# Attention's last body and the stretch behind it, with and without identity products

## The chip, the cores and the metric

The kernel runs on one core of a Trainium2 chip. The metric is device time in microseconds. Three runs of the kernel before took 544.23, 541.16 and 542.5 us, with a median of 542.5 us. The engines are PE (TensorE), DVE (VectorE), ACT (ScalarE), POOL (GpSimd) and SP, which issues most of the DMAs.

## The reference, cut to what matters

```python
def reference(x, ...):                                # x: [8, 256] token ids, width 192
    h = tok_ref(x)                                    # embedding, single-head mixer, MLP, two norms
    h = h + attn_ref(layernorm(h))                    # 12 heads of 16
    h = h + ffn_ref(layernorm(h))                     # two-level soft mixture of 8 x 4 experts

def attn_ref(x):
    qkv = (x @ qkv_w.T + qkv_b).reshape(B, N, 3, H, D).transpose(2, 0, 3, 1, 4)
    q, k, v = rms_norm(qkv[0], q_norm_w), rms_norm(qkv[1], k_norm_w), qkv[2]
    w = softmax(einsum('bhnd,bhmd->bhnm', q, k) / sqrt(D))
    out = einsum('bhnm,bhmd->bhnd', w, v).transpose(0, 2, 1, 3).reshape(B, N, C)
    return out @ proj_w.T + proj_b
```

## The kernel before, in words

Everything is in float32. The program is three blocks, one after the other: the token mixer with the attention (`mixer_and_attention`), the slots and the dispatch of the mixture (`slots_and_dispatch`), and the 32 experts (`experts`). Every engine has its own instruction list, written out by hand, and the engines meet at semaphores. Between two blocks all five engines wait for each other.

The attention works through the 8 sequences in 8 bodies (`body(n)`, n from 0 to 7). A sequence has 12 heads, in three quads of four. For each half quad PE makes a product of queries and keys for the row maxima (L615), DVE takes the maxima out of it (L1152), and PE makes the scores (L622), whose maximum is already taken off by a 17th row. PE turns the maxima (L637), ACT takes the exponentials (L927 for one half quad and L931 for the other), and PE mixes the values with them (L654). A product's banks are free again only when DVE or ACT has read them, so one group of products follows the next at the pace of DVE's maxima or ACT's exponentials. In bodies 0 to 6, PE fills that time with the front of a later sequence. In body 7 no later sequence is left.

Behind body 7 comes a tail for sequence 7 alone. It is one chain: scores, exponential, scores, exponential, mix (L654), copy on ACT (L936), six transposes (`turn_out`, L664), division on DVE (L1164 and L1168), four transposes (`turn_mixed`, L673), copy on ACT (L941), the output projection (`project`, L683), and the residual sum and its statistics on DVE and ACT (L1175 to L1186, L947 and L950).

SP's list has one duty at the end of the block. It waits for the last projection and for three other semaphores, and then clears 53 semaphores one by one (L100). After that it joins the other engines at the end of the block (L117).

`keep_busy` (L108 to L111) issues products of the identity matrix with itself, 128 by 128, into a bank that nobody reads. A float32 product is two instructions on PE. `warm(n, first, last)` issues `first` of them in body 0 and `last` of them in body 7. Other calls stand in the mixer (18), ahead of body 0 (11), between the steps of the tail (4, 4, 4, 4, 3 and 10) and in the next block (3, 16 and 4): 107 products in all.

The next block begins on PE with three transposes (`turn(0)`, L1448), three identity products, three transposes (`turn(1)`), and the logits of sequence 0 (L1466, 16 instructions).

Of the kernel before, what the change touches and what calls it, by code (L numbers as in the profile page):

```python
# [22 lines left out]
BATCH, SEQ, DIM = 8, 256, 192  # L23
# [84 lines left out]
def keep_busy(nc, g, bank, count):  # L108

    for _ in range(count):  # L110
        nc.tensor.matmul(g.ps[bank][:, 0:P], g.ident[:, :], g.ident[:, :], start=True, stop=True)  # L111


def mixer_and_attention(nc, g):

    g.next_stage()
    with ExitStack() as ctx:  # L117
# [60 lines left out]
        def norms(i, which):  # L178

            return 2 * i + which + 1  # L180
# [36 lines left out]
        MAXES, SCORES, OUT, FRONT = (0, 1), (2, 3), (4, 5), (6, 7)  # L217
# [151 lines left out]
        def _(pe):  # L369
# [271 lines left out]
            def mix(n, q):  # L641
                pe.wait_ge(S["exped"], 2 * (QUADS * n + q) + 2)
                if q == 0:
                    pe.wait_ge(S["v_kept"], n + 1)
                    if n:
                        pe.wait_ge(S["divided"], n)
                if q == 2 and n == 0:
                    pe.wait_ge(tok["stats_kept"], norms(LAST, 1))
                if q == 2 and n:
                    pe.wait_ge(S["added"], n)  # L650
                bank = g.ps[OUT[q // 2]]
                for m in range(TPS):
                    for j in range(QH):
                        last = nc.tensor.matmul(  # L654
                            bank[32 * j:32 * j + 32, (q % 2) * SEQ:(q % 2 + 1) * SEQ],
                            val[n % 2][:, m, QH * q + j, :], prob[j // 2][:, j % 2, m, :],
                            start=(m == 0), stop=(m == TPS - 1))
                last.then_inc(S["mixed"], 1)

            def turn_out(n):  # L660
                pe.wait_ge(S["out_kept"], n + 1)
                for t in range(TPS):
                    for q in range(QUADS):
                        last = nc.tensor.transpose(g.ps[OUT[t]][:, q * P:(q + 1) * P],  # L664
                                                   out_t[:, q, t * P:(t + 1) * P], g.ident[:, :])
                last.then_inc(S["out_turned"], 1)

            def turn_mixed(n):
                pe.wait_ge(S["divided"], n + 1)
                flat_mixed = mixed[:, :, :, :].rearrange("p t h d -> p t (h d)")  # L670
                for c in range(2):
                    for t in range(TPS):
                        last = nc.tensor.transpose(  # L673
                            g.ps[OUT[1]][0:HALF, c * SEQ + t * P:c * SEQ + (t + 1) * P],
                            flat_mixed[:, t, c * HALF:(c + 1) * HALF], g.ident[:, :])
                last.then_inc(S["mixed_turned"], 1)

            def project(n):
                pe.wait_ge(S["mixed_kept"], n + 1)
                for t in range(TPS):  # L680
                    for c in range(2):
                        k = HALF + c
                        last = nc.tensor.matmul(g.ps[OUT[1]][:, t * DIM:(t + 1) * DIM],  # L683
                                                mixed_t[0:k, c, t * P:(t + 1) * P],
                                                g.t["proj_t"][0:k, c, :], start=(c == 0), stop=(c == 1))
                last.then_inc(S["projected"], 1)

            def warm(n, first, last):

                if n == 0 and first:  # L690
                    pe.wait_ge(tok["stats_kept"], norms(LAST, 1))
                    keep_busy(nc, g, OUT[1], first)
                if n == BATCH - 1 and last:
                    keep_busy(nc, g, FRONT[0], last)

            def body(n):
                fill, stat, prev = n + 1 < BATCH, n + 2 < BATCH, n > 0
# [8 lines left out]
                else:  # L706
                    pe.wait_ge(S["fill_kept_s"], 2 * n + 2)
                warm(n, 0, 5)
                scores_and_maxima((n - 1, 2, 1) if prev else None, nxt(0))
                if fill:  # L710
                    make_qk_rest(n + 1)
                warm(n, 0, 3)
                turn_max(n, 0)
                warm(n, 2, 0)
                if prev:
                    mix(n - 1, 2)
# [50 lines left out]
            for n in range(BATCH):  # L767
                body(n)
            scores_and_maxima((BATCH - 1, 2, 0), None)
            keep_busy(nc, g, 0, 4)  # L770
            scores_and_maxima((BATCH - 1, 2, 1), None)
            keep_busy(nc, g, 0, 4)
            mix(BATCH - 1, 2)
            keep_busy(nc, g, 0, 4)
            turn_out(BATCH - 1)
            keep_busy(nc, g, 0, 4)
            turn_mixed(BATCH - 1)
            keep_busy(nc, g, 0, 3)
            project(BATCH - 1)
            keep_busy(nc, g, 0, 10)  # L780

        @block.scalar
        def _(act):
# [1578 lines left out]
```

## Time and profile before

| | |
|---|---|
| median of three runs | 542.5 us |
| the three runs | 544.23, 541.16, 542.5 us |
| profiled execution, its own time | 544.31 us |
| its span, first to last instruction | 542.5 us |
| mean granted TensorE clock | 0.994 |
| PE busy | 514.5 us (95%) |
| DVE busy | 315.8 us (58%) |
| ACT busy | 252.8 us (47%) |
| POOL busy | 103.1 us (19%) |

The attention's bodies run from about 117 us of the span to 257.9 us, the tail to 269.2 us. The next block's first instruction starts at 273.14 us, the experts' at 397.88 us. The profiled execution takes 1.8 us more than its span, which is the time ahead of the first instruction and behind the last. A busy PE in the profile includes the identity products.

### The profile page before, as it was taken

How to read it: one execution, taken by the hardware profiler on the slowest of the kernel's cores; microseconds unless marked ns; L12 is line 12 of the kernel's file. 1: busy time of each engine (PE TensorE's matmuls, PEld its weight loads, DVE VectorE, ACT ScalarE, POOL GpSimd, SP SyncE). 2: the span in 40 equal slices, each digit the busy share in tenths (PEclk: the TensorE clock that was granted, in tenths of full speed). 3: DMA queues.
4: the chain of work that ended last, by engine and by line, in shares of the span. 5: the costliest groups of instructions: out<-in, count | busy, mean ns of one | idle time of the engine just before them, and what ended most of it. 6: DMA issues, size and time to landing. Idle time of an engine off the chain costs nothing. (4 is left out here: it accounts for less than half of the span.)

```text
span 542.5 us, 13583 instructions
## 1 busy us (share of the span) xinstructions
PE 514.5 (95%) x5421; PEld 422.2 (78%) x5421; DVE 315.8 (58%) x743; ACT 252.8 (47%) x823; POOL 103.1 (19%) x189
## 2 busy tenths in 40 slices
PE   6999999999999999999978899899989999999996
PEld 5888888965565566666867664588889999999985
DVE  3348679677767767755227866577723444434443
ACT  1244343456566567644347658757732322323220
POOL 6380000021042144041223760000100000000000
PEclk9999999999999999999989999899999999999999
DMA  6190000000000000000074000600059999899733
GB/s 246 29 316 3 2 0 1 2 1 1 1 1 2 1 1 1 2 2 1 1 306 160 2 2 2 234 1 2 1 221 408 314 359 383 319 325 310 196 53 123
DMA packets 20722, 58.80 MB, mean 108 GB/s; under 512 B 3042, under 2 KB 9796, under 8 KB 20548
## 3 DMA queue, kind: packets, MB, share of 16 engines
q1 hardware_dynamic: 14756, 49.47, 24.7%
q0 software_dynamic: 1056, 4.33, 4.2%
q10 hardware_dynamic: 4848, 4.13, 2.6%
q8 instruction: 43, 0.70, 0.6%
q14 instruction: 19, 0.16, 0.1%
HBM read 53.21 MB, written 4.33 MB: 106 GB/s over the span
## 5 line engine op out<-in xcount | busy, mean ns | idle before, releaser
L1152 DVE TENSOR_REDUCE qk<-banks 128x4 f32<-128x1024 f32 x48 | 58.8, 1225 | 39.5 <-PE banks L615 39.5
L2092 PE MATMUL banks<-slots_t,w 64*128 64x128 f32 x1344 | 80.7, 272 | 1.1 <-PEq L1323 1.1
L2092 PEld LDWEIGHTS banks<-slots_t,w 64*128 64x128 f32 x1344 | 79.1, 188 | 1.5 <-issue 1.3
L615 PE MATMUL banks<-qk_t 16*128 16x256 f32 x384 | 54.4, 400 | 2.6 <-DVE qk L1152 2.4
L622 PE MATMUL banks<-qk_t 17*128 17x256 f32 x384 | 54.4, 400 | 0.0
L615 PEld LDWEIGHTS banks<-qk_t 16*128 16x128 f32 x384 | 33.2, 184 | 20.3 <-issue 13.7
L2195 DVE TENSOR_REDUCE tokens<-banks 128x192 f32<-128x384 f32 x32 | 17.8, 557 | 47.2 <-PE banks L2123 47.2
L931 ACT ACTIVATE wk_t<-banks 128x512 f32<-128x512 f32 x48 | 26.1, 595 | 32.8 <-PE banks L622 32.8
L355 POOL TENSOR_TENSOR qk<-qk,att_rms 128x384 f32<-128x384 f32 x14 | 11.4, 837 | 150.6 <-ACT att_rms L903 150.6
L2165 ACT ACTIVATE yn_t<-banks,b_sb 128x128 f32<-128x128 f32 x64 | 18.3, 368 | 45.3 <-PE banks L2092 45.3
L2165 ACT ACTIVATE tokens<-banks,b_sb 128x128 f32<-128x128 f32 x64 | 18.3, 369 | 44.7 <-PE banks L2092 44.7
L927 ACT ACTIVATE wq_t<-banks 128x1024 f32<-128x1024 f32 x24 | 24.6, 1025 | 26.0 <-PE banks L622 25.6
L2123 PE MATMUL banks<-w,yn_t 64*128 64x192 f32 x384 | 35.3, 323 | 1.0 <-DVE yn_t L2185 1.0
L622 PEld LDWEIGHTS banks<-qk_t 17*128 17x128 f32 x384 | 32.8, 184 | 1.0 <-DVE qk_t L1157 0.4
L2123 PEld LDWEIGHTS banks<-w,yn_t 64*128 64x128 f32 x384 | 30.8, 187 | 1.2 <-issue 1.2
L111 PE MATMUL banks<-ident 128*128 128x128 f32 x214 | 28.1, 279 | 0.0
L111 PEld LDWEIGHTS banks<-ident 128*128 128x128 f32 x214 | 25.5, 192 | 2.6 <-issue 2.6
L2185 DVE SCALAR_TENSOR_TENSOR yn_t<-banks,b_sb,tokens 128x128 f32<-128x128 f32 x64 | 18.0, 344 | 16.1 <-ACT tokens L2165 16.1
L2214 POOL DMA_DIRECT2D yn_all<-rows_scratch x7 | 3.5, 500 | 120.7 <-DMA rows_scratch<-tokens 120.7
L2185 DVE SCALAR_TENSOR_TENSOR yn_t<-banks,b_sb,yn_t 128x128 f32<-128x128 f32 x64 | 18.0, 344 | 13.0 <-ACT yn_t L2165 13.0
L654 PE MATMUL banks<-wq_t,val 128*32 128x256 f32 x192 | 25.4, 385 | 0.1
L654 PE MATMUL banks<-wk_t,val 128*32 128x256 f32 x192 | 25.4, 385 | 0.0
(251 smaller groups left out, 1128.6 us busy)
## 6 DMA issues: line engine op xcount, KB each, us to landing
w<-in_w SPq DMA_DIRECT2D x28, 768.0 KB, 10.6
w<-in_w2e SPq DMA_DIRECT2D x24, 384.0 KB, 11.9
yn_t<-in_w SPq DMA_DIRECT2D x4, 768.0 KB, 10.3
yn_t<-in_w2e SPq DMA_DIRECT2D x8, 384.0 KB, 12.5
rows_scratch<-tokens ACTq DMA_DIRECT2D x28, 96.0 KB, 7.5
yn_all<-rows_scratch POOLq DMA_DIRECT2D x7, 384.0 KB, 9.8
w<-in_w_slot SPq DMA_DIRECT2D x4, 576.0 KB, 8.9
w_slot<-in_w_slot SPq DMA_DIRECT2D x3, 576.0 KB, 5.7
```

Of the source, the lines that this page charges most:

```text
L111: nc.tensor.matmul(g.ps[bank][:, 0:P], g.ident[:, :], g.ident[:, :], start=True, stop=True)
L615: last_best = nc.tensor.matmul(g.ps[MAXES[hh]][:, half * SEQ:(half + 1) * SEQ], g.qk_t[bn_ % 2][row:row + HDIM, bq, 0, half * P:(half + 1) ...
L622: last_score = nc.tensor.matmul(g.ps[SCORES[hh]][:, half * SEQ:(half + 1) * SEQ], g.qk_t[n % 2][row:row + HDIM + 1, q, 1, half * P:(half + ...
L654: last = nc.tensor.matmul(bank[32 * j:32 * j + 32, (q % 2) * SEQ:(q % 2 + 1) * SEQ], val[n % 2][:, m, QH * q + j, :], prob[j // 2][:, j % ...
L927: nc.scalar.activation(prob[u][:, :, :, :].rearrange("p a b n -> p (a b n)"), flat(SCORES[0], SCORES[1] + 1), ACT.Exp).then_inc(S["exped"], 1)
L931: nc.scalar.activation(prob[u][:, hh, :, :].rearrange("p b n -> p (b n)"), g.ps[SCORES[hh]][:, :], ACT.Exp).then_inc(S[done], 1)
L1152: nc.vector.tensor_reduce(to, flat(MAXES[0], MAXES[1] + 1).rearrange("p (h t n) -> p h t n", h=2, n=SEQ), AX.X, ALU.max, negate=True).then ...
L2092: return nc.tensor.matmul(bank[:, j * P:(j + 1) * P], g.w1[n % BUFS][rows, first + j * P:first + (j + 1) * P], x, start=start, stop=stop, ...
L2123: last = nc.tensor.matmul(out_bank(n, half)[:, 0:DIM], act_t[n % 2][rows, j * P:(j + 1) * P], g.w2[e][rows, j, :], start=(j == 0), stop=(j ...
L2165: nc.scalar.activation(gelu[n % 2][:, j * P:(j + 1) * P], gate_bank(n)[:, j * P:(j + 1) * P], ACT.Gelu_apprx_tanh, bias=g.t["b1"][:, n, HB ...
L2185: nc.vector.scalar_tensor_tensor(out=act_t[n % 2][:, j * P:(j + 1) * P], in0=value_bank(n)[:, j * P:(j + 1) * P], scalar=g.t["b1"][:, n, j ...
L2195: nc.vector.tensor_reduce(rows[n % ROWS][:, :], g.psum[:, first:first + 2, 0:DIM].rearrange("p b d -> p d b"), AX.X, ALU.add).then_inc(S[" ...
```

## The change

`warm` no longer issues anything in body 7, and the six calls of `keep_busy` in the tail are gone. The products in body 7 were 5, 3, 2, 2 and 4 (16 products), those of the tail 29. So 45 of the 107 identity products are left out, 90 instructions on PE with their weight loads. The other 62 stay, the three in the next block among them. No other engine's list changes, and no wait is added or removed. What the kernel computes is unchanged.

```diff
                 if n == 0 and first:
                     pe.wait_ge(tok["stats_kept"], norms(LAST, 1))
                     keep_busy(nc, g, OUT[1], first)
-                if n == BATCH - 1 and last:
-                    keep_busy(nc, g, FRONT[0], last)
...
             for n in range(BATCH):
                 body(n)
             scores_and_maxima((BATCH - 1, 2, 0), None)
-            keep_busy(nc, g, 0, 4)
             scores_and_maxima((BATCH - 1, 2, 1), None)
-            keep_busy(nc, g, 0, 4)
             mix(BATCH - 1, 2)
-            keep_busy(nc, g, 0, 4)
             turn_out(BATCH - 1)
-            keep_busy(nc, g, 0, 4)
             turn_mixed(BATCH - 1)
-            keep_busy(nc, g, 0, 3)
             project(BATCH - 1)
-            keep_busy(nc, g, 0, 10)
```

PE's list at the start of body 7, before. L615 and L622 are the products for maxima and scores, L637 turns the maxima, and L111 is `keep_busy`:

```order
L622 MATMUL banks<-qk_t 128x256 x2
L111 MATMUL banks<-ident 128x128 x5
L615 MATMUL banks<-qk_t 128x256 x2
L622 MATMUL banks<-qk_t 128x256 x2
L615 MATMUL banks<-qk_t 128x256 x2
L622 MATMUL banks<-qk_t 128x256 x2
L111 MATMUL banks<-ident 128x128 x3
L637 MATMUL banks<-ident,qk 128x128 x2
```

The same place with the change:

```order
L622 MATMUL banks<-qk_t 128x256 x2
L615 MATMUL banks<-qk_t 128x256 x2
L622 MATMUL banks<-qk_t 128x256 x2
L615 MATMUL banks<-qk_t 128x256 x2
L622 MATMUL banks<-qk_t 128x256 x2
L637 MATMUL banks<-ident,qk 128x128 x2
```

Two rows of identity products are gone, and the groups on either side of them stand next to each other, in the old order.

PE's list from the end of the last mix over the end of the block (L117) into the next block, before:

```order
L654 MATMUL banks<-wk_t,val 32x256 x2
L111 MATMUL banks<-ident 128x128 x4
L664 MATMUL banks<-ident,wv_t 128x128 x6
L111 MATMUL banks<-ident 128x128 x4
L673 MATMUL banks<-ident,w 96x128 x4
L111 MATMUL banks<-ident 128x128 x3
L683 MATMUL banks<-proj_t_sb,xt 128x192 x4
L111 MATMUL banks<-ident 128x128 x10
L117 UNCONDITIONAL_BRANCH
L1438 UNCONDITIONAL_BRANCH
L1448 MATMUL banks<-ident,tokens 128x128 x3
L111 MATMUL banks<-ident 128x128 x3
```

The same place with the change, where the next block's lines have moved up by eight:

```order
L654 MATMUL banks<-wk_t,val 32x256 x2
L664 MATMUL banks<-ident,wv_t 128x128 x6
L673 MATMUL banks<-ident,w 96x128 x4
L683 MATMUL banks<-proj_t_sb,xt 128x192 x4
L117 UNCONDITIONAL_BRANCH
L1430 UNCONDITIONAL_BRANCH
L1440 MATMUL banks<-ident,tokens 128x128 x3
L111 MATMUL banks<-ident 128x128 x3
```

Between the projection and the next block's first transposes PE now has nothing to do.

## Rows read from the trace of the kernel before

**Rows 1.** The page: TensorE's granted clock in 40 slices, in tenths.
```profile
PEclk9999999999999999999989999899999999999999
```

**Rows 2.** The identity products' line: duration in ns as min/median/max.
```profile
L111 PE MATMUL banks<-ident x214: 272/275/377, 90.4 to 393.3; 128*128 128x128 f32 x107
```

**Rows 3.** Timeline, start of body 7: start, duration, engine, instructions, [idle before <-releaser].
```profile
241.15 1.38 PE L111 MATMUL banks<-ident 128*128 128x128 f32 x10
241.25 1.23 DVE L1152 TENSOR_REDUCE qk<-banks 128x4 f32<-128x1024 f32 x1 [0.31 <-PE banks L615]
...
242.62 0.48 PE L615 MATMUL banks<-qk_t 16*128 16x256 f32 x2
```

**Rows 4.** Timeline of the tail and the border to the next block.
```profile
259.04 1.02 ACT L927 ACTIVATE wq_t<-banks 128x1024 f32<-128x1024 f32 x1 [2.28 <-PE banks L622]
...
260.12 1.13 PE L622 MATMUL banks<-qk_t 17*128 17x256 f32 x8
...
264.43 0.87 PE L664 MATMUL banks<-ident,wv_t 128*128 128x128 f32 x6
...
266.29 0.64 PE L673 MATMUL banks<-ident,w 128*96 128x128 f32 x4
...
266.97 0.58 ACT L941 COPY xt<-banks 96x512 f32<-96x512 f32 x1 [2.60 <-PE banks L673]
267.60 1.57 PE L683 MATMUL banks<-proj_t_sb,xt 96*128 96x192 f32 x8
269.01 2.39 PE L111 MATMUL banks<-ident 128*128 128x128 f32 x20
...
271.07 0.20 ACT L950 ACTIVATE out_factor<-att_out_log 128x2 f32<-128x2 f32 x1
...
273.16 0.52 PE L1448 MATMUL banks<-ident,tokens 128*128 128x128 f32 x3 [1.75 <-PEq L117]
```

**Rows 5.** Waits of SP's queue, 266 to 274 us: total, times, longest.
```profile
SPq L100 <- PE banks L683: 1.6, 1, 1.6
...
SPq L117 <- PEq L117: 0.2, 1, 0.2
```

**Rows 6.** Timeline at the border to the experts.
```profile
396.92 0.59 ACT L1782 COPY slots_t<-banks 128x512 f32<-128x512 f32 x1 [2.28 <-PE banks L1638]
...
397.93 0.38 PE L2092 MATMUL banks<-slots_t,w 64*128 64x128 f32 x2 [1.06 <-PEq L1323]
```

**Rows 7.** Windows: length, busy us of PE, PEld, DVE, ACT, POOL, clock, DMA.
```profile
257.90:269.20 11.30, 11.07 (x94) 8.95 (x91) 1.72 (x6) 3.88 (x7) 3.00 (x3) 1.00 0.01 1
...
274.00:275.00 1.00, 1.00 (x9) 0.86 (x8) 0.00 (x0) 0.25 (x1) 1.00 (x2) 0.80 0.86 189
...
277.00:278.00 1.00, 1.00 (x9) 0.78 (x8) 0.12 (x1) 0.00 (x0) 0.00 (x0) 0.50 1.01 383
278.00:279.00 1.00, 0.41 (x3) 0.17 (x2) 0.64 (x2) 0.56 (x2) 0.00 (x0) 1.00 1.00 406
...
305.30:312.10 6.80, 5.07 (x47) 4.03 (x44) 5.85 (x18) 3.77 (x21) 4.74 (x13) 1.00 0.00 0
```

**Rows 8.** Window of the tail, line L111 on PE alone: busy us, clock.
```profile
257.90:269.20 11.30, 5.55 (x40) 1.00 0.01 1
```

**Rows 9.** Timeline of the next block's first 9 us.
```profile
275.62 1.06 PE L1466 MATMUL banks<-phi_t,slots_t 128*128 128x128 f32 x4
...
279.81 0.44 PE L1482 MATMUL banks<-ident,slots_t 128*128 128x128 f32 x2 [1.40 <-ACT slots_t L1701]
...
280.53 0.61 PE L1466 MATMUL banks<-phi_t,slots_t 128*128 128x128 f32 x4
```

**Rows 10.** Timeline of PE, 346 to 350 us.
```profile
346.06 1.06 PE L1568 MATMUL banks<-ident,slots_t 128*128 128x128 f32 x8 [0.35 <-ACT se_t L1751]
...
349.91 1.94 PE L1568 MATMUL banks<-ident,slots_t 128*128 128x128 f32 x8 [2.35 <-ACT se_t L1751]
```

**Rows 11.** Timeline of PE near the kernel's end.
```profile
534.19 5.42 PE L2131 MATMUL banks<-yn_all,mix_t 128*64 128x192 f32 x64 [1.68 <-DMA yn_all<-tokens]
```

## The prediction, made before the changed kernel was run

> **What bounds the kernel now.** I read the page's row of granted clocks first. It shows that TensorE loses its full clock twice, once in slice 21 and once in slice 26 [rows 1]. The first place is the start of the block behind the attention. So the question is two-sided: what PE time do the identity products take from the path, and what does the clock do without them?
>
> Next I read the timeline of body 7 and of the tail, engine by engine, and asked for each PE group what released it. At the start of body 7, DVE's maxima run from 241.25 us for 1.23 us, so they end at 242.48. PE's next group starts at 242.62. The five identity products issued at 241.15 end at 242.53, inside that wait [rows 3]. In the tail the scores at 260.12 start when ACT's exponential ends (259.04 + 1.02 = 260.06), and the projection at 267.60 starts when ACT's copy ends (266.97 + 0.58 = 267.55) [rows 4]. All of body 7 and of the tail reads this way: groups follow each other at DVE's or ACT's pace, and the identity products stand in the gaps.
>
> The border between the blocks looked at first as if PE's last ten products set it. They end at 271.40, and PE starts again 1.75 us later [rows 4]. But SP says otherwise. It waited 1.6 us for the last projection before its clears, and only 0.2 us at the end of the block [rows 5]. The wait of 0.2 us means that SP came last. From the projection's end (269.17) to 272.9 is 3.7 us for 53 clears, 70 ns each. The border to the experts, where SP clears nothing at the end, supports this. There ACT's last copy ends at 397.51 and PE starts at 397.93, 0.4 us later [rows 6], and not 1.75 or 1.9. So the next block starts 4.0 us after the end of the projection (269.17 to 273.16), whatever PE does in between.
>
> **What is removed.** 45 products go, 90 instructions. The 20 behind the projection take 2.39 us with one latency of 0.275 us in it [rows 2, 4], so one costs PE (2.39 - 0.275) / 19 = 0.111 us, and all 90 cost 10.0 us of PE's time. On the path they cost nothing, by the releases above. The bounds: at four places in body 7 the products end within 0.1 us of the next PE group's start, so up to 0.3 us may come back in all. I take 0. The ten behind the projection lie wholly beside SP's clears, and if that cover were gone they would be worth the 2.2 us of the third rival.
>
> **What the clock does.** This is where the change costs. The rows before give four idles of PE: 1.40 us [rows 9] and 1.68 us [rows 11] left the clock at full; behind 1.75 us [rows 4] and 2.35 us [rows 10] it was at half, 1.2 GHz in place of 2.4. With the change PE idles from 269.17 to 273.16, 4.0 us in one piece and longer than any of the four. So the next block will start at half clock, nearly for certain.
>
> The tail ahead of the projection is less clear. Of its 11.3 us PE is busy 11.07, of which 5.55 are identity products [rows 7, 8]. Without them PE works for half of the time, in pieces of 0.6 to 1.6 us with idles of 0.7 to 1.3 us. No single idle is as long as 1.75 us. A stretch with a busy share of 5.07 in 6.80 us (75%) kept the full clock [rows 7], but no row shows one at 50% with this mix. So the clock may fall before the projection or not.
>
> The Trainium skill, on the page "TensorE: Matmul & The Clock Gate", section "Part 1: The HAM clock gate (the 'warmup' mystery)", says that the low clock is the default and that activity is what releases it. Its part on "A second HAM failure mode: psum-queue depth-cycling" says that frequent short idles between groups of matmuls are enough to make the clock swing. By that rule the tail's fall is certain, and the tail's term below would be 2.2 in place of 1.4; no row of this kernel shows a fall behind short idles alone.
>
> **Price of the tail at half clock.** Eight instructions of one form take 1.06 us at full and 1.94 us at half, a factor of 1.83 [rows 10]. The projection's eight instructions occupy PE for 1.41 us (267.60 to 269.01) [rows 4], so they gain 0.83 x 1.41 = 1.2 us. The six transposes (0.87, of which 0.7 streams) gain 0.6, the four (0.64, of which 0.48 streams) gain 0.4 [rows 4]. All three stand on the path with nothing beside them, and behind the projection SP waits, so the 4.0 us move as a whole. The sum is 0 if the clock holds up to the projection's end, 1.2 if it falls ahead of the projection alone, and 2.2 if it falls ahead of the six. I take 1.4, because most of the idle lies just ahead of the projection. DVE and ACT work on between PE's pieces at their own speed.
>
> **Price of the next block's start.** PE works alone from 273.16 to 278.0: transposes, three identity products, transposes and the first logits. In the profiled run the slice from 274 us has a mean clock of 0.80, so the clock fell at 274.6, and it was back at 278.0 [rows 7]: 3.4 us at half. Four instructions of the logits took 1.06 us in it and 0.61 us once the clock was back [rows 9]. So these 3.4 us cost a little under half of themselves, 1.6 us. The whole stretch is then 1.4 + 1.8 = 3.2 us at full and 5.9 at half. With the change it starts at half. The loss lies between 0 (the low time lies wholly in the 4.0 us of idle) and 2.7 us (it lasts to the end of the stretch). The fall seen in the profiled run ended after 3.4 us of work. I take 1.9, a little above its 1.6, because here the work starts low and no row says when the clock comes back from a longer idle.
>
> **Body 7.** Its first products are now followed by idles of 1.4 to 1.6 us with 1.1 us of work between them. A fall there would slow one or two score groups and a mix, about 1.0 us. I give it 1 in 5, so 0.2 us.
>
> **The sum.** The profiled run took 544.31 us (span 542.5) and has already paid the first fall. A run like it would take 544.31 - 1.6 + 1.9 + 1.4 + 0.2 = 546.2 us. The three runs spread over 3.07 us, close to the price of two falls of 1.6, and the lowest, 541.16, is then a run without either. The median, 542.5, lies 1.8 us below the profiled time, so it has about one. For a typical run I start at the lowest, 541.2, add half of the second fall, 0.8, which the change doesn't touch, and the three terms of 3.5 in all: 545.5 us. That is 3.0 us or 0.55% over the median.
>
> The Trainium skill, on the same page, section "What's actually happening", puts the cost of regaining the clock under 1% of a typical kernel's span. That would be at most 5.4 us here; the price of 1.6 us for one fall agrees, and the sum of 3.5 stays below it.
>
> **The rivals.** First, the clock holds through the tail and falls only in the 4.0 us behind the projection. For it: no idle of the tail reaches 1.75 us. Against it: half of the tail's PE work is gone. The time is 541.2 + 0.8 + 1.9 = 543.9 us, no measurable change.
>
> Second, the clock falls in body 7 already and again through the tail, and spends little of the last 30 us of the block at full. For it: PE's load from 240 to 269 us drops by 70 instructions. Against it: DVE and ACT set the pace there and hide part of a slower PE. It takes the tail at 2.2 and body 7 at 1.0 to 1.7, so 541.2 + 0.8 + 1.9 + 2.2 + 1.3 = 547.4 us.
>
> Third, on the other side: the block's end waits for PE, not for SP, and the next block follows PE's last product by the 1.75 us seen now. Then the ten products cost 271.40 - 269.17 = 2.2 us, and without a fall of the clock the kernel takes 542.5 - 2.2 = 540.3 us. It decides if the next block starts less than 3.5 us behind the projection. Against it stands SP's wait of only 0.2 us [rows 5].
>
> **How the numbers follow.** Forecast 0.50 (544.0 to 547.2 us), first rival 0.22 (542.8 to 544.8), second 0.22 (546 to 549), third 0.06. What this kernel's measurement can tell from no change is about 0.5%, 2.7 us, so slower means above 545.2 and faster below 539.8. Slower gets 0.30 of the forecast's 0.50 and 0.21 of the second rival's, 0.51. Faster gets 0.03, from the third. The rest is 0.46. The range reaches from 543.0, inside the first rival, to 548.5, inside the second, and leaves out some 2 in 10.
>
> **What would show it.** In the changed kernel's trace: PE's groups in body 7 still start right behind DVE's or ACT's end (0.14 us behind at the group of 242.62); the next block starts 4.0 us after the projection's end; the granted clock is 0.50 at the next block's first transposes; the projection's eight instructions span about 2.6 us, not 1.4. The prediction is wrong if the clock is full at the projection and at the block's start, if the block's start moves closer to the projection, or if the identity products' places close up.

## The result, and the profile after

The changed kernel takes 555.68 us (median of four runs, 552.44 to 557.76) against 543.21 us of before in four runs. The ratio is 1.0247, with a 95% interval from 1.0218 to 1.0275. The change makes the kernel slower by 2.5%, some 12.5 us. The forecast was 545.5 us, with a range up to 548.5. Throughout, a ratio and its median leave out runs more than 1.5% above the fastest of their kernel, and the text gives their times.

The profiled execution of the changed kernel took 552.44 us, its span is 550.6 us, and it is the quickest of the four. The page shows the same instructions as before less the 90, and a clock row below 9 in four slices, down to 5, where [rows 1] had two slices at 8:

```profile
PE 513.5 (93%) x5331; PEld 417.4 (76%) x5331; DVE 315.8 (57%) x743; ACT 252.8 (46%) x823; POOL 103.0 (19%) x189
...
PEclk9999999999999999997659999989999999999999
```

PE is busy for 513.5 us, 1.0 us less than before, though work of 10 us was taken away. The rest of the work has become longer. Windows over body 7, the tail and the border show where (start and end, length, busy us of PE, PEld, DVE, ACT and POOL, granted clock, DMA):

```profile
241.00:245.00 4.00, 1.96 (x32) 1.17 (x24) 2.34 (x5) 1.97 (x5) 1.55 (x2) 1.00 0.00 0
245.00:250.00 5.00, 4.82 (x37) 2.56 (x38) 1.46 (x3) 1.70 (x4) 1.44 (x2) 0.55 0.00 0
250.00:255.00 5.00, 5.00 (x35) 3.08 (x37) 3.31 (x5) 2.21 (x4) 0.00 (x0) 0.50 0.00 0
...
260.00:265.00 5.00, 3.31 (x34) 1.98 (x34) 1.75 (x6) 2.33 (x5) 0.31 (x1) 1.00 0.00 0
...
270.00:275.00 5.00, 3.33 (x13) 2.49 (x12) 0.87 (x2) 0.58 (x1) 0.00 (x0) 0.50 0.00 0
...
285.00:290.00 5.00, 3.60 (x30) 2.98 (x29) 1.25 (x4) 2.01 (x9) 0.61 (x1) 0.85 1.02 411
```

The clock is at half from 245.5 to 255.8 us, in the middle of body 7. It is full until 266.0, and at half again until 286.5, through the tail and over the border. That is 30.7 us at 1.2 GHz, where the kernel before had 3.4 us in the same stretch. A timeline of the same stretch, to be read against [rows 3, 4, 9]:

```profile
241.84 1.23 DVE L1144 TENSOR_REDUCE qk<-banks 128x4 f32<-128x1024 f32 x1 [0.31 <-PE banks L615]
...
243.22 0.48 PE L615 MATMUL banks<-qk_t 16*128 16x256 f32 x2 [1.41 <-DVE qk L1144]
...
264.23 1.13 PE L622 MATMUL banks<-qk_t 17*128 17x256 f32 x8 [1.12 <-ACT wq_t L919]
...
269.40 1.54 PE L664 MATMUL banks<-ident,wv_t 128*128 128x128 f32 x6 [0.92 <-ACT wv_t L928]
...
271.93 1.09 PE L673 MATMUL banks<-ident,w 128*96 128x128 f32 x4 [0.99 <-DVE w L1160]
...
273.69 2.93 PE L683 MATMUL banks<-proj_t_sb,xt 96*128 96x192 f32 x8 [0.67 <-ACT xt L933]
...
280.61 0.88 PE L1440 MATMUL banks<-ident,tokens 128*128 128x128 f32 x3 [3.99 <-PEq L117]
...
288.26 0.44 PE L1474 MATMUL banks<-ident,slots_t 128*128 128x128 f32 x2 [1.40 <-ACT slots_t L1693]
```

The first two rows show that the products did stand in a wait. DVE ends at 243.07, PE's group starts 0.15 us later, and the idle of 1.41 us ahead of it is where five products were. Each row's start less that of its counterpart before gives the loss step by step, in us:

| start of | before | after | later by | added since the row above |
|---|---|---|---|---|
| second group of body 7 | 242.62 | 243.22 | 0.60 | (older than the change's place) |
| tail's second scores | 260.12 | 264.23 | 4.11 | 3.51, body 7 |
| six transposes | 264.43 | 269.40 | 4.97 | 0.86, the mix |
| four transposes | 266.29 | 271.93 | 5.64 | 0.67, the six |
| projection | 267.60 | 273.69 | 6.09 | 0.45, the four |
| next block | 273.16 | 280.61 | 7.45 | 1.36, the projection |
| its first transposes of dispatch | 279.81 | 288.26 | 8.45 | 1.00, besides the 1.6 that before paid here |

The span is longer by 8.1 us in the end (550.6 against 542.5). SP's waits at the block's end are the counterpart of [rows 5]:

```profile
SPq L100 <- PE banks L683: 3.0, 1, 3.0
...
SPq L117 <- PEq L117: 0.2, 1, 0.2
```

SP waits for the projection, clears its semaphores and comes last again: at the block's end it waits only 0.2 us.

### The profile page after: what moved, and what is told of

It is laid out like the page before. It is cut to its first block and busy times, and to the rows that moved or that the text cites. A ratio compares the mean times of both kernels' runs of the same rounds, so it can differ in the third digit from the quotient of the medians.

```text
span 550.6 us, 13404 instructions
## 1 busy us (share of the span) xinstructions
PE 513.5 (93%) x5331; PEld 417.4 (76%) x5331; DVE 315.8 (57%) x743; ACT 252.8 (46%) x823; POOL 103.0 (19%) x189
## 5 line engine op out<-in xcount | busy, mean ns | idle before, releaser
L615 PE MATMUL banks<-qk_t 16*128 16x256 f32 x384 | 56.2, 411 | 3.7 <-DVE qk L1144 3.6
L622 PE MATMUL banks<-qk_t 17*128 17x256 f32 x384 | 56.2, 411 | 1.1 <-ACT wq_t L919 1.1
L615 PEld LDWEIGHTS banks<-qk_t 16*128 16x128 f32 x384 | 34.1, 189 | 22.7 <-issue 16.1
L622 PEld LDWEIGHTS banks<-qk_t 17*128 17x128 f32 x384 | 33.7, 189 | 2.3 <-ACT wq_t L919 1.5
L654 PE MATMUL banks<-wq_t,val 128*32 128x256 f32 x192 | 27.7, 413 | 1.2 <-ACT wk_t L923 1.2
L654 PE MATMUL banks<-wk_t,val 128*32 128x256 f32 x192 | 27.7, 413 | 0.0
L550 PE MATMUL banks<-qkv_w_sb,w_t 128*128 128x384 f32 (+1 forms) x64 | 19.1, 420 | 0.0
L341 POOL TENSOR_SCALAR centred<-h,out_mv,out_factor 128x192 f32<-128x192 f32 x14 | 14.0, 1010 | 25.2 <-ACT out_factor L942 25.2
```

The source lines that it names most:

```text
L550: last = nc.tensor.matmul(g.ps[banks[t]][:, 0:cols.stop - cols.start], x_t[:, 2 * t, :], g.t["qkv_w"][:, 2 * t, cols], start=True, stop=False)
L615: last_best = nc.tensor.matmul(g.ps[MAXES[hh]][:, half * SEQ:(half + 1) * SEQ], g.qk_t[bn_ % 2][row:row + HDIM, bq, 0, half * P:(half + 1) ...
L622: last_score = nc.tensor.matmul(g.ps[SCORES[hh]][:, half * SEQ:(half + 1) * SEQ], g.qk_t[n % 2][row:row + HDIM + 1, q, 1, half * P:(half + ...
L654: last = nc.tensor.matmul(bank[32 * j:32 * j + 32, (q % 2) * SEQ:(q % 2 + 1) * SEQ], val[n % 2][:, m, QH * q + j, :], prob[j // 2][:, j % ...
```

## The experiments

The theory after the result was this: the whole loss is TensorE's clock, and the work of the identity products, not their mere presence, kept it up. The rivals were that body 7's fall was a chance of one run, that the idle behind the projection is what counts, that the length or place of PE's instructions matters, and that any busy PE keeps its clock. All kernels are the kernel before with one edit, and the cuts shown are shortened. Where a product is replaced by something else, that happens at the 45 places of the change alone, in a helper of its own (L117 in those kernels); the other 62 products stay as they are. What the kernel before does without any change has to be known first. It ran 52 times beside the experiments. One run took 1747 us at full clock and is left out. Of the other 51, 34 had a mean clock of 0.999 or more, with a median of 541.3 us, 9 of about 0.997 took 542.7, and 8 below 0.995 took 544.0. So a typical run of before has no fall at all, and against such a run the changed kernel's 555.68 us is 14.4 us more.

**Body 7 keeps its products, the tail's go.**

```diff
-            keep_busy(nc, g, 0, 4)          # and 4, 4, 4, 3, 10: all six calls of the tail
```

> Body 7 keeps its 16 identity products, the tail's 29 are left out. Theory A (all of the loss is TensorE's clock, and body 7's thin work is where it starts): the clock stays full until some 260 us, is low over most of the stretch from the tail to the next block's first logits; 543 + 4 to 6 = 547 to 549 us. Rival B (the first fall comes from the tail and the 4.0 us of idle, body 7's fall in the profile was a chance of that run): about as slow as the kernel with the change, 553 to 556 us.

Measured: 546.61 us, ratio 1.0083 (1.0051 to 1.0115). Windows of its profile:

```profile
240.00:260.00 20.00, 19.75 (x218) 13.50 (x216) 11.50 (x22) 8.63 (x15) 3.00 (x3) 1.00 0.01 2
264.00:280.00 16.00, 9.44 (x45) 7.00 (x38) 2.29 (x7) 2.36 (x5) 3.07 (x4) 0.50 0.08 21
```

No fall in body 7, and the clock at half over the tail and the border. The theory's place is right, and its price a little high: over the 541.3 us of a run without a fall, the tail's products are worth some 5 us.

**The tail keeps its products, body 7's go.**

```diff
-                if n == BATCH - 1 and last:
-                    keep_busy(nc, g, FRONT[0], last)
```

> Body 7 runs without its 16 identity products, the tail keeps its 29. Theory A: the clock falls at some 245 us as in the changed kernel, stays low for one stretch of body 7 and is full again over the tail and the border as before; 543 + 4 to 7 = 547 to 550 us. Rival B: no fall in body 7, 543 us, no change.

Measured: 547.91 us (three runs, 547.32 to 549.37), ratio 1.0102 (1.0061 to 1.0144). A fourth run took 560.06 us with a mean clock of 0.963.

```profile
246.00:255.00 9.00, 9.00 (x68) 5.23 (x64) 3.87 (x6) 3.38 (x5) 0.50 (x1) 0.50 0.00 0
258.00:277.00 19.00, 16.42 (x138) 12.65 (x137) 4.44 (x14) 5.71 (x12) 3.01 (x3) 1.00 0.00 1
```

The fall in body 7 is there again, at the same place and as long, and the tail and the border run at full clock. It is no chance of one run. The run at a clock of 0.963 was not profiled; 2 x 0.037 x 558.3 gives some 41 us at half clock for it. So the same kernel can also stay low far longer than the profile shows, and why is open.

**Only the last ten go.**

```diff
             project(BATCH - 1)
-            keep_busy(nc, g, 0, 10)
```

> Only the ten identity products behind the projection are left out, so that PE has one idle of 4.0 us there. Both theories: the clock is half at the next block's start, the border itself stays 4.0 us long; the price is the term of 1.9 us that the prediction had for it less the fall that the kernel before has in part of its runs, so 544 to 545 us. If the block's end waited for PE: 541 us.

Measured: 543.88 us, ratio 1.0034 (1.0012 to 1.0056). Timeline of PE in its profile:

```profile
267.71 1.57 PE L683 MATMUL banks<-proj_t_sb,xt 96*128 96x192 f32 x8
273.27 0.87 PE L1447 MATMUL banks<-ident,tokens 128*128 128x128 f32 x3 [3.99 <-PEq L117]
...
280.67 0.44 PE L1481 MATMUL banks<-ident,slots_t 128*128 128x128 f32 x2 [1.40 <-ACT slots_t L1700]
```

From the projection's start to the next block is 5.56 us, and before it was 5.56 too (267.60 to 273.16). The ten products cover an idle that costs nothing by itself, and SP's clears set the border. The next block's first step takes 7.40 us (273.27 to 280.67), against 6.65 in [rows 4, 9] and 7.65 in the changed kernel.

**Each product as two transposes.**

```diff
-        nc.tensor.matmul(g.ps[bank][:, 0:P], g.ident[:, :], g.ident[:, :], start=True, stop=True)
+        nc.tensor.transpose(g.ps[bank][:, 0:P], g.ident[:, :], g.ident[:, :])     # 2 * count times
```

> All 45 products stay in place, but each as two transposes of the identity matrix in place of its two matmul instructions: PE is as busy in the trace, with another kind of work. If PE's busy time is what keeps the clock up: 543 us, no change. If transposes don't keep it up: the clock falls as in the changed kernel, 553 to 557 us, though PE is never idle for longer than before. A cost of the missing instructions other than the clock (their time, their place) would give 543 us too.

Measured: 541.67 us, ratio 0.9999 (0.9977 to 1.0020).

```profile
240.00:280.00 40.00, 36.05 (x355) 26.82 (x356) 14.72 (x32) 15.69 (x34) 9.00 (x9) 1.00 0.13 46
```

```profile
273.98 0.52 PE L1454 MATMUL banks<-ident,tokens 128*128 128x128 f32 x3 [1.80 <-PEq L123]
...
349.18 1.06 PE L1574 MATMUL banks<-ident,slots_t 128*128 128x128 f32 x8 [2.34 <-ACT se_t L1757]
```

The clock is full over all 40 us. Transposes of 128 by 128 hold it as well as products do: eight of the ten runs have a mean clock of 0.999 or more. The same step of the next block takes 5.10 us here (273.98 to 279.08), so that is its length at full clock; before's own 6.65 had 1.55 us of the fall in it. The last two rows are the places of before's two falls [rows 4, 10]. The idles of PE are as long here, 1.80 and 2.34 us against 1.75 and 2.35, and the clock stays full behind both. So the length of an idle alone doesn't say whether the clock falls.

**Each product on 16 rows.**

```diff
-        nc.tensor.matmul(g.ps[bank][:, 0:P], g.ident[:, :], g.ident[:, :], start=True, stop=True)
+        nc.tensor.matmul(g.ps[bank][:, 0:P], g.ident[0:HDIM, :], g.ident[0:HDIM, :], start=True, stop=True)
```

> All 45 products stay in place with as many instructions and columns, but each uses only the first 16 rows of the identity matrix, as the attention's score products do, in place of 128. If what keeps the clock up is that PE has instructions to stream: 542 to 543 us, no change. If the score products' small part of the array is the reason why the clock fell in body 7, which was PE's main work there: the clock falls as in the changed kernel, 550 to 557 us. A cost by time or place of the instructions would give no change.

Measured: 563.04 us, ratio 1.0382 (1.0355 to 1.0409), slower than with no products at all. A window, then the timeline of PE and ACT in the tail:

```profile
244.00:298.00 54.00, 51.95 (x284) 38.68 (x282) 10.34 (x21) 11.63 (x21) 7.70 (x8) 0.50 0.09 30
```

```profile
268.33 2.08 PE L628 MATMUL banks<-qk_t 17*128 17x256 f32 x8
...
271.53 0.80 PE L628 MATMUL banks<-qk_t 17*128 17x256 f32 x2
...
276.65 2.07 PE L117 MATMUL banks<-ident 16*128 16x128 f32 x8
276.79 0.80 ACT L942 COPY wv_t<-banks 128x768 f32<-128x768 f32 x1 [2.05 <-PE banks L660]
278.65 1.54 PE L670 MATMUL banks<-ident,wv_t 128*128 128x128 f32 x6
```

PE is busy for 51.95 of 54 us, and the clock is at half throughout. So a busy PE does not keep its clock; what it works on decides. Where the clock is at half, the products also come onto the path. ACT's copy behind the mix ends at 277.59, but the six transposes start at 278.65, when the four products ahead of them are through. In the changed kernel, which has no products there, the same transposes start 0.06 us after ACT's copy (269.34 to 269.40). The products ahead of the four transposes, of the projection and of the border hold PE in the same way, by 0.8 to 1.0 us each. From the mix to the next block it takes 17.72 us (274.79 to 292.51), and 14.07 in the changed kernel (266.54 to 280.61), both at half clock. Between two score groups it is not so: from 268.33 to 271.53 is 3.20 us, where before had 2.26 (257.86 to 260.12), and the score group itself is longer by as much (2.08 against 1.13). So this kernel loses more than the changed one for two reasons, the products on the path and the 54 us at half clock in place of 30.7 in this stretch.

**Half of the products.**

```diff
-                warm(n, 0, 5)       # 5, 3, 2, 2, 4 in body 7; 4, 4, 4, 4, 3, 10 in the tail
+                warm(n, 0, 3)       # 3, 1, 1, 1, 2 in body 7; 2, 2, 2, 2, 1, 5 in the tail
```

> About half of the products stay at every place: 3, 1, 1, 1 and 2 in body 7, and 2, 2, 2, 2, 1 and 5 in the tail (22 of 45). Theory A (clock, with a level of work below which it falls): either all falls are avoided (542 to 543 us) or part of them, at the tail and the border first, with 544 to 549 us. If the loss went with the number of missing products it would be half of 12.5: 549 us.

Measured: 549.49 us, ratio 1.0152 (1.0120 to 1.0183). The number is what the linear rival said, but the profile doesn't support it. Body 7 keeps the full clock with 8 of its 16 products:

```profile
240.00:262.00 22.00, 20.01 (x213) 12.91 (x213) 11.24 (x21) 9.74 (x17) 3.61 (x4) 1.00 0.01 1
263.00:269.00 6.00, 5.62 (x32) 3.98 (x33) 0.86 (x2) 0.99 (x2) 1.39 (x2) 0.50 0.00 0
```

Falls come in the tail and at the border only, 10.2 us in all. The rest of the loss stands 200 us later, in the experts. PE's waits there, and one of them in the timeline:

```profile
PE banks L2123 <- issue: 1.7, 2, 1.1
...
PE banks L2092 <- issue: 0.6, 1, 0.6
```

```profile
469.47 1.08 PE L2123 MATMUL banks<-w,yn_t 64*128 64x192 f32 x10 [1.09 <-issue]
```

PE stops for 1.09 us amid a run of products for nothing that the profile shows. There are three such waits, which add up to 2.3 us. From the experts' first product to the start of their last step it takes 140.0 us (399.03 to 539.03), and before took 136.26 (397.93 to 534.19), at full clock in both.

**Half of the products, and PE's list as long as before.** The other 23 stay as products of one column.

```diff
+    for _ in range(count):
+        nc.tensor.matmul(g.ps[bank][:, 0:1], g.ident[:, :], g.ident[:, 0:1], start=True, stop=True)
```

> The kernel with half of the products (22 of 45), with the other 23 as products of 1 column, so that PE's list is as long as before. With half of the products alone the median was 549.5 us, with 10.5 us at half clock and, in the experts, six waits of PE in its own queue of 0.6 to 1.1 us each, 3.7 us in all, which none of the other kernels but one has. If those waits hang on where the shorter list puts the experts' instructions: they are gone here, and 549.5 - 3.7 = 545.8 us is left, the clock's part. If they are the products' or the clock's doing: 549 to 550 us again.

Measured: 546.7 us (seven runs, 544.2 to 549.7), ratio 1.0087 (1.0055 to 1.0119). Three more of the ten runs took 559.5 to 560.6 us. The list of waits has three of them in the kernel with the short list (2.3 us in all), not six with 3.7 us as the expectation says, and two other kernels have one or two. The profiled run took 545.04 us, with as much time at half clock as the kernel with the short list (10.2 us), and no wait of the kind "issue" in the experts, which take 136.2 us (398.75 to 534.93) and not 140.0. The two profiled runs differ by 4.1 us. Runs with the same mean clock agree: at 0.991 the short list took 548.75, 549.15 and 549.83 us, the long one 545.02 and 545.04. So 3 to 4 us of the 549.5 were not the clock's. They go with the length of PE's list, and so with the place of the experts' instructions in it. That the cause is the fetching of instructions is a guess; no run tests it.

The three runs of 559.5 to 560.6 us have a mean clock of 0.963, which gives some 41 us at half clock (2 x 0.037 x 558). So with half of the products the clock also stayed low far longer, in three runs of ten, and the profiled run with its 10.2 us shows only the milder case. Why one run goes one way and the next the other is open.

**Only body 7's first eight go.**

```diff
-                warm(n, 0, 5)
+                warm(n, 0, 0)
...
-                warm(n, 0, 3)
+                warm(n, 0, 0)
```

> Only the first eight products of body 7 (5 and 3, in the first two gaps) are left out. In the changed kernel the clock fell at 245.5 us, right behind these gaps, so theory A expects most of body 7's loss from them: a fall at some 245 us, back after one stretch of 3.4 us or so since the later products are there, 544 to 546 us. If body 7 as a whole has to be thin before the clock falls: 542.6 us, no change.

Measured: 547.26 us, ratio 1.0097 (1.0068 to 1.0126), with runs from 544.4 to 550.0.

```profile
240.00:244.00 4.00, 2.37 (x36) 1.50 (x32) 2.31 (x7) 1.55 (x4) 1.14 (x2) 1.00 0.01 4
245.00:257.00 12.00, 12.00 (x83) 7.68 (x84) 4.19 (x7) 3.37 (x5) 0.93 (x1) 0.50 0.01 1
```

```profile
242.63 0.48 PE L615 MATMUL banks<-qk_t 16*128 16x256 f32 x2 [1.41 <-DVE qk L1152]
...
265.87 1.13 PE L622 MATMUL banks<-qk_t 17*128 17x256 f32 x8
```

Two bare gaps at the start of body 7 are enough for the fall. In the 12 us from 245 PE is busy without a break, with four of the eight products left among its work, and stays at half. The expectation that the later products bring the clock back after 3.4 us was wrong: it took 13.7. From body 7's second group to the tail's second scores it is 23.24 us here (242.63 to 265.87), where before had 17.50 (242.62 to 260.12). That is 5.7 us more, against 3.5 us where all 16 products are gone. So in this run the products that are left didn't help once the clock was low. The four that stand in the low stretch take about twice as long, and the fall lasts 13.7 us in place of 10.2. The runs of 544.4 and 545.0 us have a mean clock of 0.994 and 0.993 against this run's 0.987, so the fall isn't as long in all of them.

**Only the tail's 19 ahead of the projection go.**

```diff
-            keep_busy(nc, g, 0, 4)          # 4, 4, 4, 4 and 3; the 10 behind the projection stay
```

> Only the tail's 19 products ahead of the projection are left out. Body 7 keeps its 16 and the ten behind the projection stay. The kernel without any of the tail's 29 had 546.6 us, that without the last ten alone 543.9. Theory A: the clock falls at some 262 us and stays low up to the projection or the border; the prediction's term for the tail, 1.4 (at most 2.2), is too small, since scores, mix and both latencies of each step slow down too: 541.3 + 3 to 4 = 544.3 to 545.3 us. If the term of 1.4 was right: 542.7 us.

Measured: 549.64 us, ratio 1.0136 (1.0082 to 1.0190), more than expected. Timeline of PE:

```profile
259.92 1.26 PE L622 MATMUL banks<-qk_t 17*128 17x256 f32 x8 [1.12 <-ACT wq_t L922]
...
269.51 2.93 PE L683 MATMUL banks<-proj_t_sb,xt 96*128 96x192 f32 x8 [0.67 <-ACT xt L936]
...
276.43 0.52 PE L1443 MATMUL banks<-ident,tokens 128*128 128x128 f32 x3 [0.74 <-PEq L117]
```

The tail is as the theory has it: from the scores to the next block is 16.51 us here (259.92 to 276.43), 13.04 before (260.12 to 273.16), so it costs 3.5 us. The rest lies elsewhere: a fall of 6.8 us at 353 us in the next block, where the profiled run of before has one of 3.4 us, and experts of 139.1 us (401.13 to 540.26) in place of 136.3, with two waits of the kind "issue" (0.9 and 0.6 us), as with half of the products. The median alone would have misled.

**Each product with one column.**

> All 45 products stay in place as instructions, with their weight loads, but each streams 1 column in place of 128. PE's list is as long as before and there is almost no work in the products. Theory A (the work kept the clock up): the clock falls in body 7 and in the tail as in the changed kernel, 552 to 558 us. If the length of PE's list or the weight loads made the difference: 541 to 543 us.

The edit is the one-column product above, for all 45. Measured: 562.3 us, ratio 1.0376 (1.0322 to 1.0430). First the start of body 7, then two windows, ahead of the fall and in it:

```profile
241.51 1.28 PE L117 MATMUL banks<-ident 128*128 128x1 f32 x10
```

```profile
241.00:245.00 4.00, 3.73 (x45) 2.96 (x38) 2.34 (x5) 2.19 (x5) 1.78 (x2) 0.98 0.00 0
...
245.00:295.00 50.00, 49.70 (x266) 38.16 (x267) 9.82 (x21) 10.76 (x20) 7.05 (x8) 0.50 0.04 12
```

Ten instructions of one column take 1.28 us, nearly as long as ten of 128 columns (1.38 us in [rows 3]). Each has a weight load of 128 columns beside it, which may be what sets its pace; no run separates the two. So this kernel gives PE nearly as much to do in time, at the same places and with a list as long as before. In the 4 us up to 245 PE is busy for 3.73 us, almost all of it still at full clock, where the changed kernel had 1.96, and the clock falls all the same. Then it is at half for 51 us while PE is busy 49.70 of 50. The length of the list, the places and the busy time are all excluded as what held the clock; the work in the products is left.

**More products at the two places where before can fall.**

```diff
-            keep_busy(nc, g, 0, 10)
+            keep_busy(nc, g, 0, 17)
...
             turn_logits(0)
+            keep_busy(nc, g, WEIGHTS, 9)
             turn_se2(UNITS - 1)
```

> The kernel before with 16 more products at the two places where its own trace shows a fall: 17 in place of 10 behind the projection (up to SP's last clear at 272.9 us) and 9 in PE's idle of 2.35 us at 347.6 us in the next block. Theory A: neither fall comes any more, and no product is on the path; the median comes down to the lowest runs of before, 541 to 541.5 us against 542.6. If the products were on the path: 543 to 544 us.

Measured: 542.58 us, ratio 1.0013 (1.0000 to 1.0026), so no gain. Timeline of PE, to compare with [rows 10]:

```profile
346.83 2.17 PE L111 MATMUL banks<-ident 128*128 128x128 f32 x18
349.33 1.06 PE L1568 MATMUL banks<-ident,slots_t 128*128 128x128 f32 x8 [0.33 <-ACT se_t L1752]
```

The falls are gone: all 12 runs have a mean clock of 0.999 or more, and the transposes take 1.06 us. But two in three of before's runs have no fall either, at 541.3 us, and against these the new kernel is 1.3 us slower. Where that goes was not found. In its profiled run the experts' last step starts at 531.45 us, earlier than the 531.84 of the kernel with transposes, but its span is 0.7 us longer (540.9 against 540.2). No version was faster than the kernel before.

## Why the prediction was wrong

**That the removed products were not on the path** was right. DVE's end and PE's start are 0.15 us apart with the products gone, as they were 0.14 apart with them.

**That SP's clears set the border** was right. The idle behind the projection grew to 3.99 us, and from the projection's start to the next block it was 5.56 us with and without the ten products. The third rival, a border that waits for PE, is excluded by that.

**Body 7's term of 0.2 us** is where it failed most. It measured 3.5 us in the profiled runs of the changed kernel and of the one without these products alone. The latter's profiled run takes 8.1 us more than a run without a fall. Besides the 3.5 us it has two more losses, a fall near the kernel's end (1.7 us) and 2.3 us in the experts. The prediction gave a fall in body 7 a chance of 1 in 5, and 1.0 us if it came. Both parts were wrong. The fall came in the profiled runs of all three kernels in which the first two gaps were bare. It lasted 10.2 us and more. In the changed kernel two score groups, two mixes and the transposes between them fall into it, not one or two score groups and one mix. The prediction also counted on DVE and ACT to set the pace and hide part of a slower PE. At half clock PE was busy for 5.00 of 5.00 us (the window from 250), so it set the pace itself and nothing was hidden.

The reasoning behind the chance was at fault too: it listed PE's idles in [rows 4, 9 to 11] and asked whether a single new one is longer than 1.75 us. The idle of 1.41 us in body 7 is as long as that of 1.40 us [rows 9] and shorter than that of 1.68 us [rows 11], which both kept the clock. Nor do 1.75 and 2.35 us mark a limit, since behind the idle of 1.75 us the clock was still full for another 1.4 us (273.16 to 274.6), and idles of 1.80 and 2.34 us kept the full clock in the kernel with transposes. With 16-row or one-column products there is hardly any idle, and the clock falls all the same. What PE's list ahead of the prediction also showed, and the prediction didn't use, is what PE has left to do at the start of body 7: score products on 16 and 17 rows, and nothing else, up to 0.3 us before the fall. The 75% busy stretch that kept its clock [rows 7] was work on 64 and 128 rows.

**The tail's term of 1.4 us** (at most 2.2) measured 3.3 in the changed kernel and 3.5 where the tail alone lost its products. The prediction left open whether the clock falls there before the projection. All profiled runs without the tail's 19 products had that fall, and even the upper bound of 2.2 us, for a fall ahead of the six transposes, was too low. The sum also left out the mix, 0.86 us, which falls in the same stretch. The three steps it did have came out at 0.67, 0.45 and 1.36, near the prices of 0.6, 0.4 and 1.2.

**The next block's start**, priced at 1.9 us over a full clock and at 2.7 at most, measured 7.65 - 5.10 = 2.6 us. The mechanism was right; the clock stayed low nearly to the stretch's end.

**The base of 541.2 + 0.8 us** was about right: a run without a fall takes 541.3. Half a second fall was too much, since two runs in three have none.

The sum over the fall-free run is 3.5 + 3.3 + 2.6 = 9.4 us of the 11.1 us of the profiled run; one more fall in the next block, of 3.4 us at half, is in it at 358 us and takes most of the rest. Of the other three runs of the changed kernel, one has a mean clock of 0.969 and took 553.73 us, and two have 0.956 and took 557.7; the profiled run has 0.968. So the 14.4 us of the median are accounted for stage by stage only up to the profiled run's 11.1. Both ends of the range cost about a third of a microsecond for each microsecond at half, with the time at half worked out from the mean clock: (552.44 - 541.3) over 2 x 0.032 x 550.6 = 35 us, and (557.7 - 541.3) over 2 x 0.044 x 556 = 49 us. Why the clock is low for 35 us in one run and 49 in another is open, and so is why it came back at 255.8 us in the changed kernel and not with one-column products.

The second rival, falls in body 7 and through the tail, was the right picture, at 547.4 us and a chance of 0.22. Its own price for body 7, 1.0 to 1.7 us, was less than half of what it costs, so even that picture missed the measured time by 8 us.

## What to carry to other kernels

Before taking filler work off TensorE, ask what the engine has left to do there, and on how many rows and columns, not only how long it idles. Filler that stands in waits is free only as long as the clock is full: at half clock it takes twice as long and comes onto the path. So half of the filler can cost more than none: in the profiled runs, body 7 took 2.2 us longer with eight products left than with none (23.24 against 21.01 us). And where a median and the clock disagree, compare the timelines stage by stage, because a shorter instruction list moved 3 to 4 us in a stage 200 us away.

## What the runs showed of the hardware

- TensorE kept its full clock with products or transposes of 128 rows and 128 columns in the gaps. It fell to half with products of 16 rows by 128 columns, or of 128 rows and one column, at the same places, and stayed there while PE was busy for 51.95 of 54 us and 49.70 of 50 us.
- Transposes hold the clock as products do: the ratio of the two kernels is 0.9999 (0.9977 to 1.0020).
- Idles of PE of 1.75 and 2.35 us came ahead of work at half clock in the profiled run of the kernel before, and idles of 1.80 and 2.34 us at the same places left the clock at full in that of the kernel with transposes.
- Ten float32 instructions of one column, each with a weight load of 128 columns, take 1.28 us, and ten of 128 columns 1.38 us.
- The next block starts 4.0 us after the end of the projection with the ten products and without them. SP's 53 clears fill 3.7 us of that, an estimate of 70 ns each from [rows 4, 5]. Where the ten products ran at half clock, the border waited for PE and came 4.9 us after the projection with 16 rows (287.65 to 292.51) and 4.4 us with one column (287.69 to 292.05).
- The traces showed waits of PE of 0.6 to 1.1 us amid dense products, put down to nothing, in three of the kernels with 32, 38 or 46 fewer instructions on PE. They were in none of the kernels with 16, 20, 58 or 90 fewer, and filling up the list by 46 took them away.
